# Row weights on ScalarE, and GpSimd's split of each expert's weights in pieces

## The chip, the core and the metric

The kernel runs on one core of one Trainium2 chip. The metric is the device time of one launch in microseconds (us). Three runs of the kernel before took 857.39, 860.36 and 863.71 us; their median is 860.36 us. The core has five engines that run their own instruction streams and meet through semaphores: TensorE (PE in the profile, its weight loads PEld), VectorE (DVE), ScalarE (ACT), GpSimd (POOL) and SyncE (SP), which here only issues transfers.

## The reference

Two blocks follow each other, each as `x = x + layernorm(block(layernorm(x)))`, on x of 2 x 2048 tokens by 256. The first is a gated linear attention with 16 heads. The second, around which the change is made, is a mixture of experts:

```
gate_out = x @ gate_w                       # 8 experts
top_v, top_i = top_k(gate_out, 2)           # each token goes to 2 of them
w = softmax over the two chosen, 0 elsewhere
def swiglu(x, w1, w2, w3):
    h = x @ w1
    return h * sigmoid(h) * (x @ w2) @ w3   # 256 -> 512 -> 256
out = sum over experts of swiglu(x, ew1[e], ew2[e], ew3[e]) * w[..., e]
out = out + swiglu(x, sw1, sw2, sw3)        # the shared expert
```

## The kernel before

**Two phases.** Phase A does the attention and the routing, and at its end each token's normalised row is scattered by GpSimd (L555) to a scratch in memory, sorted by expert. Phase B does the experts. It is a list of *units*: 5 shared units of 256 tokens, then 31 routed pairs (two tiles of 128 rows of one expert), 9 routed singles (one tile), and 11 more shared units. The table `tab`, written by VectorE (L1521 to L1523), tells each routed unit its expert and its first row. Experts come in rising order, about four pairs to each.

**Numbers in float16.** Each float32 matrix is kept as two float16 ones, a high and a low part, and each product is three matmuls. So each expert's weights are *split*: scaled into `wtmp_p` (L1695), copied to float16 (L1699), and the remainder computed (L1701). GpSimd does this for experts 1 to 8, 3072 columns per instruction. The scale comes from the largest weight of the expert: VectorE reduces each matrix (L1529, one per gap of its program), SyncE spreads the maxima over the partitions through memory, and VectorE's `scales` (L785 to L792) works out `w_scale`, for experts 2 and 3 in unit 2 and for 4 to 8 in unit 8.

**One unit.** TensorE turns the next unit's rows (L1269), computes the hidden layer in two halves (L1285, for a single L1305), then the output of the unit before (L1327). ScalarE takes the high part of the turned rows (`high_x`, L1386), applies SiLU (L1376), takes the high part of the gated product (`high_g`, L1369) and at the top of its next round moves output rows out of PSUM, each times its weight in `wrow` (`rows_out`, L1407). VectorE takes the low part of the rows (`low_x`, L1642), multiplies SiLU by the second product (`gated`, L1634) and takes the low part (`low_g`, L1625). The second matmul group of a half reuses the bank that `low_g` of two halves before has read.

**Row weights.** A scattered row carries its destination, the number of one of its two experts, a softmax value, and what to add to it where that number is this expert. ScalarE's `tags` (L1390, L1392) puts the destination and "number minus this expert" in `tag`. VectorE's `weights_of_rows` (L1574 to L1577) makes `wrow` of them in four small instructions, each behind the one before, right after `low_x` of the next unit.

**Queues.** SyncE loads the rows of a unit (L1206) once its expert is split and the row weights of the unit two before are written (`wrow_ready`). GpSimd scatters finished tiles back to memory (`scatter`, L1707 to L1716) in order; `ysh` has a ring of 28 tiles, so `rows_out` of tile j waits for the scatter of tile j - 28. GpSimd runs its program in written order: split 1, 2, 3, then 6 scatters after each of the splits 3 to 8, then the rest.

Of the kernel before, what the change touches and what calls it, by code (L numbers as in the profile page):

```python
# [5 lines left out]
ALU = mybir.AluOpType  # L6
# [11 lines left out]
def sandwich_kernel(nc, x, Wq, Wk, Wv, Wo, Wg, bg, gate_w, ew1, ew2, ew3, sw1, sw2, sw3, out):  # L18
    P = 128
# [19 lines left out]
    MW = KC * H  # L39
# [16 lines left out]
    with ctx:  # L56
# [167 lines left out]
        def settle(eng):  # L224


            eng.nop(nofuse=True)
# [828 lines left out]
        def sc(name, shape, dt=F32):  # L1056
            return phase_b.enter_context(nc.sbuf_tensor(name, shape, dt))
# [9 lines left out]
        second = sc("second", [P, 1])  # L1067
        chosen2 = sc("chosen2", [P, 2, 2])
        wrow = sc("wrow", [P, RT])
# [67 lines left out]
        def rows_upto(u):  # L1137

            return sum(t.tiles if t.routed else 1 for t in units[:u + 1])

        def halves_upto(u):
# [219 lines left out]
        def scalar_b(act):  # L1361
# [27 lines left out]
            def tags(t, e):  # L1389
# [3 lines left out]
                               bias=away9[:, e]).then_inc(T["tag_ready"], 1)  # L1393

            def rows_out(t, e):
                act.wait_ge(T["y_done"], t.u + 1)
# [37 lines left out]
            for u in range(ENDS):  # L1434
# [19 lines left out]
                if t is not None and t.halves == 2:  # L1454
                    high_g(t, 0)
                    silu(t, 1, e_of[u])
                    load_matrices()
                    high_g(t, 1)
            normalise_rows(C - 1)

        def vector_b(dve):
# [3 lines left out]
            def link(ins):  # L1465
                n[0] += 1
                ins.then_inc(T["late_chain"], 1)
                dve.wait_ge(T["late_chain"], n[0])
# [99 lines left out]

            def weights_of_rows(t, e):

                x = xt[t.q % 2]
                own, part, out = chosen2[:, 0, 0:t.tiles], chosen2[:, 1, 0:t.tiles], wrow[:, t.j:t.j + t.tiles]
                dve.wait_ge(T["tag_ready"], 2 * (t.q + 1))
                link(V.tensor_scalar(own, tag[:, t.j:t.j + t.tiles, 1], 0.0, None, ALU.is_equal))  # L1574
                link(V.tensor_tensor(part, own, x[:, 0:t.tiles, D + 3], ALU.mult))
                link(V.tensor_tensor(part, part, x[:, 0:t.tiles, D + 2], ALU.add))  # L1576
                V.tensor_scalar(out, part, w_scale[:, 2, e], None, ALU.mult).then_inc(T["wrow_ready"], 1)  # L1577

            def add_rows(c):
# [67 lines left out]
            for u in range(ENDS):  # L1647
# [4 lines left out]
                if prev is not None and prev.kind == "single":  # L1652
                    low_g(prev, 0)
                if following is not None and following.routed:
                    weights_of_rows(following, expert_of(dve, following))
                if waiting is not None:
# [30 lines left out]
        def pool_b(pool):  # L1687

            BETWEEN = 6

            def split(e):
                whole = W[:, e].rearrange("p m n -> p (m n)")
                if e > 1:
                    pool.wait_ge(experts_split, e - 1)
                pool.tensor_scalar(wtmp_p[:, :, :].rearrange("p m n -> p (m n)"), whole, w_scale[:, 1, e:e + 1], 1.0,  # L1695
                                   ALU.mult, ALU.mult).then_inc(T["pool_split"], 1)
                pool.wait_ge(T["pool_split"], 2 * e - 1)
                settle(pool)
                pool.tensor_copy(W16[:, e, :, 0, :], wtmp_p[:, :, :]).then_inc(T["pool_split"], 1)  # L1699
                pool.wait_ge(T["pool_split"], 2 * e)  # L1700
                pool.tensor_tensor(W16[:, e, :, 1, :], wtmp_p[:, :, :], W16[:, e, :, 0, :], ALU.subtract)\  # L1701
                    .then_inc(experts_split, 1)

            def scatter(j):
                need(pool, T["tag_ready"], 2 * (tile_unit[j].q + 1))
                need(pool, T["dest_ready"], j)
# [107 lines left out]
```

## Time and profile before

| | |
|---|---|
| three runs, median | 860.36 us |
| the profiled execution | 861.15 us |
| its span in the trace | 859.2 us |
| busy: PE, PEld | 740.7, 612.1 us |
| busy: DVE, ACT, POOL | 635.4, 415.6, 494.2 us |
| chain that ended last, by engine | PE 33%, DVE 18%, issue 5%, ACT 3%, POOL 1% |

Busy time of an engine is the time in which one of its compute instructions ran. PE is the busiest, but this is a mean over stages: phase B starts near 343 us, the routed units run from near 410 us to 752 us, and which engine sets the pace changes within them. The trace rows carry the start of an instruction, its duration, and in brackets how long its engine had been idle before and what ended the wait. The granted clock of PE is given as a share of full speed; where it is near 0.5 the clock was at 1.2 GHz, and at 1.00 it was at 2.4 GHz.

### The profile page before, as it was taken

The page shows a single profiled execution, that of the slowest core. Times are in us where ns is not written, and L with a number is a line of the kernel's source. Part 1 is how long each engine was busy: PE and PEld are TensorE (multiplying, and loading weights), DVE is VectorE, ACT ScalarE, POOL GpSimd, SP SyncE. Part 2 cuts the span into 40 slices and gives each one's busy share as a digit, 9 for nine tenths or more (in the row PEclk, how much of TensorE's full clock was granted, in tenths as well). Part 3 has the DMA queues.
Part 4 walks back from the last instruction along what each step waited for, and adds up shares of the span by engine and source line. Part 5 has one row for each costly group of instructions (what it writes and reads, how often), then busy time and mean ns, then how long its engine had stood idle before and what let it go on. Part 6 is the DMA issues. An engine that isn't in the chain of part 4 may idle for free.

```text
span 859.2 us, 25434 instructions
## 1 busy us (share of the span) xinstructions
PE 740.7 (86%) x8863; PEld 612.1 (71%) x8863; DVE 635.4 (74%) x1286; ACT 415.6 (48%) x840; POOL 494.2 (58%) x653
## 2 busy tenths in 40 slices
PE   5779989899899984867597889898999999999983
PEld 4557777787787763635486778787899985688873
DVE  4897989989998992778876766667555554547996
ACT  2645667566676542222234334433554444445553
POOL 4133335887778776689413877687534434325665
PEclk8999999999999996768799999999999999999998
DMA  7434333444453437662332111211212111217885
GB/s 245 99 80 104 102 101 82 151 120 114 137 158 108 130 109 249 208 178 74 92 106 78 51 45 57 76 45 50 76 57 76 57 51 59 79 48 219 196 169 102
DMA packets 57480, 93.24 MB, mean 109 GB/s; under 512 B 7216, under 2 KB 35760, under 8 KB 57360
## 3 DMA queue, kind: packets, MB, share of 16 engines
q1 hardware_dynamic: 40512, 60.66, 24.8%
q0 software_dynamic: 10672, 22.57, 9.7%
q10 hardware_dynamic: 6176, 8.40, 3.6%
q8 instruction: 77, 1.26, 0.6%
q14 instruction: 43, 0.35, 0.1%
HBM read 59.60 MB, written 32.01 MB: 107 GB/s over the span
## 4 chain that ended last, share of the span: by engine, by line
PE 33%; DVE 18%; issue 5%; ACT 3%; POOL 1%; DVEq 1%; DMA 1%; ACTq 0%; POOLq 0%
PE bank L1285 19%; PE bank L1327 10%; DVE chosen L1576 4%; DVE wpart L1529 2%; PE bank L1305 2%; DVE bank L1634 2%; ACT gh L1369 2%; DVE gl L1625 1%; DVE wtmp_p L1588 1%; DVE chosen L1574 1%; PE bank L1269 1%; DVEq L1168 1%; DVE wmax L786 1%; DVE stc L1601 1%; ACT xh L1386 1%
## 5 line engine op out<-in xcount | busy, mean ns | idle before, releaser
L1285 PE MATMUL bank<-xh,W 128*128 128x256 f16 x1504 | 271.9, 282 | 47.9 <-DVE gl L1625 41.0
L1285 PE MATMUL bank<-xl,W 128*128 128x256 f16 x752 | 211.8, 282 | 1.5 <-issue 1.5
L1285 PEld LDWEIGHTS bank<-xh,W 128*128 (+1 forms) x1504 | 151.7, 101 | 76.1 <-issue 41.5
L1716 POOL DMA_INDIRECT yt_scratch<-ysh,dest x71 | 76.4, 1076 | 161.8 <-ACT ysh L1407 124.6
L1369 ACT ACTIVATE gh<-bank 128x512 f16<-128x512 f32 x103 | 61.3, 595 | 223.0 <-DVE bank L1634 214.5
L1327 PE MATMUL bank<-W,gh 128*128 (+1 forms) x824 | 141.3, 276 | 3.0 <-DVE gl L1625 1.9
L1625 DVE TENSOR_TENSOR gl<-bank,gh 128x512 f16<-128x512 f32 x103 | 71.0, 689 | 66.9 <-ACT gh L1369 66.3
L1327 PE MATMUL bank<-W,gl 128*128 (+1 forms) x412 | 113.8, 276 | 0.3 <-issue 0.3
L555 POOL DMA_INDIRECT xs_scratch<-xn_all,posi x64 | 88.5, 1382 | 27.5 <-issue 13.9
L1634 DVE SCALAR_TENSOR_TENSOR bank<-sl,w_scale,bank 128x512 f32<-128x512 f32 x94 | 70.8, 753 | 35.5 <-PE bank L1285 19.5
L607 PE MATMUL bank<-xnT,wT 128*128 128x256 f32 x384 | 94.2, 397 | 2.3 <-ACT xnT L369 2.3
L1327 PEld LDWEIGHTS bank<-W,gh 128*128 128x128 f16 x824 | 81.4, 99 | 16.3 <-issue 2.9
L607 PEld LDWEIGHTS bank<-xnT,wT 128*128 128x128 f32 x384 | 72.5, 195 | 18.9 <-issue 5.8
L1285 PEld LDWEIGHTS bank<-xl,W 128*128 (+1 forms) x752 | 75.9, 101 | 12.2 <-issue 1.9
L1376 ACT ACTIVATE sl<-bank,w_scale 128x512 f32<-128x512 f32 x103 | 70.6, 685 | 19.0 <-PE bank L1285 11.8
L850 DVE TENSOR_TENSOR_SCAN W<-W,diag 128x1024 f32<-128x1024 f32 x32 | 72.1, 2281 | 10.2 <-DMA W<-gate_scratch 9.9
L1642 DVE TENSOR_TENSOR xl<-bank,xh 128x512 f16<-128x512 f32 (+1 forms) x40 | 25.2, 631 | 37.5 <-ACT xh L1386 35.7
L711 PE MATMUL bank<-W 64*32 64x64 f32 x2048 | 35.3, 224 | 16.0 <-DVE W L870 9.1
L1701 POOL TENSOR_TENSOR W<-wtmp_p,W 128x3072 f16<-128x3072 f32 x8 | 48.4, 6048 | 0.7
L1327 PEld LDWEIGHTS bank<-W,gl 128*128 128x128 f16 x412 | 40.8, 99 | 6.4 <-issue 1.3
L420 ACT ACTIVATE W<-qT,qmask 128x512 f32<-128x512 f32 x64 | 42.4, 711 | 5.5 <-DVE qT L904 5.5
L1407 ACT ACTIVATE ysh<-bank,wrow 128x256 f32<-128x256 f32 x71 | 30.2, 471 | 30.4 <-PE bank L1327 27.1
(205 smaller groups left out, 1412.6 us busy)
## 6 DMA issues: line engine op xcount, KB each, us to landing
W<-gate_scratch SPq DMA_DIRECT2D x64, 256.0 KB
ysh<-yt_scratch SPq DMA_DIRECT2D x16, 512.0 KB, 4.6
xt<-xs_scratch SPq DMA_DIRECT2D x31, 260.0 KB
W<-in_L_ffn_ew_dram ACTq DMA_DIRECT2D x15, 512.0 KB, 3.7
W<-in_L_ffn_ew_dram SPq DMA_DIRECT2D x9, 512.0 KB, 8.3
x_in<-in_L_attn_x_dram SPq DMA_DIRECT2D x16, 256.0 KB, 3.6
out_dram<-x SPq DMA_DIRECT2D x16, 256.0 KB
xT_scratch<-xn2T SPq DMA_DIRECT2D x16, 256.0 KB
```

What stands on the lines that cost most here:

```text
L420: act.activation(free3(qx[s % 2][:, c]), free3(qT[s % 2][:, :, :, :]), ACT.Copy, scale=qmask[:, c:c + 1]).then_inc(S["qx_ready"], 1)
L555: pool.indirect_dma_start(xs_d[:, :], bass.IndirectOffsetOnAxis(ap=posi[:, s, b * TOPK + k:b * TOPK + k + 1], axis=0), xn2[s % XB][:, b, : ...
L607: last = mm(dst[:, g * B * P:(g + 1) * B * P], wT[:, n, k, g * P:(g + 1) * P], xnT[s % 2][:, k, :], start=(k == 0), stop=(k == KC - 1))
L850: V.tensor_tensor_scan(dec[:, w, :], gbc[s % 2][:, w, :], free2(diag[:, :, :]), 0.0, ALU.mult, ALU.add).then_inc(S["decay_ready"], 1)
L1285: last = mm(dst[n % 2][:, i * R:(i + 1) * R], W16[:, e, m, s, at:at + P], a[:, k, :], start=(k == 0 and s == 0 and a is x_h), stop=(k == K ...
L1327: last = mm(pYB[t.u % 2][:, r * D:(r + 1) * D], g[:, i, r, :], W16[:, e, 2, s, c * D:(c + 1) * D], start=(c == 0 and r == 0 and a is gh an ...
L1369: act.activation(gh[t.u % 2][h][:, :], (pH1 if t.kind == "single" else pH2)[n % 2][:, :], ACT.Copy)\
L1376: act.activation(sl[n % 2][:, :], pH1[n % 2][:, :], ACT.Silu, scale=w_scale[:, 0, e])\
L1625: V.tensor_tensor(gl[t.u % 2][h][:, :], (pH1 if t.kind == "single" else pH2)[n % 2][:, :], gh[t.u % 2][h][:, :], ALU.subtract).then_inc(T[ ...
L1634: V.scalar_tensor_tensor((gg if t.kind == "single" else pH2)[n % 2][:, :], sl[n % 2][:, :], w_scale[:, 1, e], pH2[n % 2][:, :], ALU.mult, ...
L1701: pool.tensor_tensor(W16[:, e, :, 1, :], wtmp_p[:, :, :], W16[:, e, :, 0, :], ALU.subtract)\
L1716: pool.indirect_dma_start(yt_d[:, :], bass.IndirectOffsetOnAxis(ap=dest[:, j:j + 1], axis=0), ysh[:, ETILES + j % RING, :], None).then_inc ...
```

## The change

`weights_of_rows` goes from VectorE to ScalarE, as five or four small ACTIVATE instructions: |number - e|, then max(0, 1 - that), which is 1 where the number is this expert and 0 else, then one multiply-add for each tile, then the product with the expert's scale. They stand at the end of ScalarE's round, behind the last `high_g`. The counts on `tag_ready` are adapted (`tags_upto`). GpSimd's split is cut: three scalings and three casts of 1024 columns, six subtractions of 512. `BETWEEN` goes from 6 to 2.

```
+            def weights_of_rows(t, e):
+
+                x, done = xt[t.q % 2], tags_upto(t.q - 1)
+                far, own, part = chosen2[:, 0, 0:t.tiles], chosen2[:, 1, 0:t.tiles], chosen2[:, 2, 0:t.tiles]
+                act.wait_ge(T["tag_ready"], done + 2)
+                need(act, T["wrow_ready"], t.q)
+                act.activation(far, tag[:, t.j:t.j + t.tiles, 1], ACT.Abs).then_inc(T["tag_ready"], 1)
+                act.wait_ge(T["tag_ready"], done + 3)
+                act.activation(own, far, ACT.Relu, scale=-1.0, bias=1.0).then_inc(T["tag_ready"], 1)
+                act.wait_ge(T["tag_ready"], done + 4)
+                for r in range(t.tiles):
+                    act.activation(part[:, r:r + 1], x[:, r, D + 3:D + 4], ACT.Identity, scale=own[:, r:r + 1],
+                                   bias=x[:, r, D + 2:D + 3]).then_inc(T["tag_ready"], 1)
+                act.wait_ge(T["tag_ready"], tags_upto(t.q))
+                act.activation(wrow[:, t.j:t.j + t.tiles], part, ACT.Copy, scale=w_scale[:, 2, e])\
+                   .then_inc(T["wrow_ready"], 1)
...
                     high_g(t, 1)
+                if following is not None and following.routed:
+                    weights_of_rows(following, e_of[u + 1])
...
-            def weights_of_rows(t, e):
-
-                x = xt[t.q % 2]
-                own, part, out = chosen2[:, 0, 0:t.tiles], chosen2[:, 1, 0:t.tiles], wrow[:, t.j:t.j + t.tiles]
-                dve.wait_ge(T["tag_ready"], 2 * (t.q + 1))
-                link(V.tensor_scalar(own, tag[:, t.j:t.j + t.tiles, 1], 0.0, None, ALU.is_equal))
-                link(V.tensor_tensor(part, own, x[:, 0:t.tiles, D + 3], ALU.mult))
-                link(V.tensor_tensor(part, part, x[:, 0:t.tiles, D + 2], ALU.add))
-                V.tensor_scalar(out, part, w_scale[:, 2, e], None, ALU.mult).then_inc(T["wrow_ready"], 1)
...
-            BETWEEN = 6
+            BETWEEN = 2
...
-                pool.tensor_scalar(wtmp_p[:, :, :].rearrange("p m n -> p (m n)"), whole, w_scale[:, 1, e:e + 1], 1.0,
-                                   ALU.mult, ALU.mult).then_inc(T["pool_split"], 1)
...
-                pool.tensor_copy(W16[:, e, :, 0, :], wtmp_p[:, :, :]).then_inc(T["pool_split"], 1)
...
-                pool.tensor_tensor(W16[:, e, :, 1, :], wtmp_p[:, :, :], W16[:, e, :, 0, :], ALU.subtract)\
-                    .then_inc(experts_split, 1)
+                for m in range(3):
+                    pool.tensor_scalar(wtmp_p[:, m, :], W[:, e, m], w_scale[:, 1, e:e + 1], 1.0,
+                                       ALU.mult, ALU.mult).then_inc(T["pool_split"], 1)
+                for m in range(3):
+                    pool.wait_ge(T["pool_split"], done + 3 + m)
+                    settle(pool)
+                    pool.tensor_copy(W16[:, e, m, 0, :], wtmp_p[:, m, :]).then_inc(T["pool_split"], 1)
+                for m in range(3):
+                    pool.wait_ge(T["pool_split"], done + 4 + m)
+                    for k in range(2):
...
+                        pool.tensor_tensor(W16[:, e, m, 1, half], wtmp_p[:, m, half], W16[:, e, m, 0, half],
+                                           ALU.subtract).then_inc(experts_split if last else T["pool_split"], 1)
```

On ScalarE, the round of an early pair, from `high_g` of its second half to `high_x` of the unit after the next; before:

```order
L1369 ACTIVATE gh_1<-bank 128x512
L1407 ACTIVATE ysh<-bank,wrow 128x256 x2
L1168 TENSOR_LOAD tab
L1168 ISA x2
L1386 ACTIVATE xh<-bank 128x512
```

and with the change:

```order
L1373 ACTIVATE gh_1<-bank 128x512
L1405 ACTIVATE chosen<-tag 128x2
L1407 ACTIVATE chosen<-chosen 128x2
L1410 ACTIVATE chosen<-xt,chosen 128x1 x2
L1413 ISA
L1413 ACTIVATE wrow<-chosen,w_scale 128x2
L1428 ACTIVATE ysh<-bank,wrow 128x256 x2
L1172 TENSOR_LOAD tab
L1172 ISA x2
L1390 ACTIVATE xh<-bank 128x512
```

The weights' instructions now stand between `high_g` and the moving out of rows, ahead of `high_x`. On GpSimd, from the split of expert 3 to that of expert 4, with the change:

```order
L1707 TENSOR_SCALAR wtmp_p<-W,w_scale 128x1024 x3
L1712 CAST W<-wtmp_p 128x1024 x3
L1720 TENSOR_TENSOR W<-wtmp_p,W 128x512 x6
L1726 TENSOR_SCALAR second<-tag 128x1
L1729 TENSOR_SCALAR dest<-tag,spare,second 128x1
L1735 DMA yt_scratch<-ysh,dest 9216x256
L1726 TENSOR_SCALAR second<-tag 128x1
L1729 TENSOR_SCALAR dest<-tag,spare,second 128x1
L1735 DMA yt_scratch<-ysh,dest 9216x256
```

Before, a split was three instructions of 3072 columns, and six scatters stood where two stand now.

## Rows read from the trace of the kernel before

**Rows 1.** Windows: busy us (and count) per engine, PE clock, DMA share, GB/s.
```profile
380.00:420.00 40.00, 25.67 (x184) 19.57 (x182) 34.85 (x30) 7.35 (x14) 36.44 (x12) 0.80 0.26 74
464.00:610.00 146.00, 131.25 (x1136) 114.67 (x1137) 99.84 (x138) 60.70 (x140) 108.98 (x105) 0.95 0.19 56
610.00:700.00 90.00, 90.00 (x826) 81.12 (x825) 47.17 (x99) 43.60 (x97) 37.74 (x66) 1.00 0.21 64
```
**Rows 2.** Timeline, split of expert 4: start us, us, engine, line, operation.
```profile
470.85 2.83 POOL L1695 TENSOR_SCALAR wtmp_p<-W,w_scale 128x3072 f32<-128x3072 f32 x1
...
476.65 6.01 POOL L1701 TENSOR_TENSOR W<-wtmp_p,W 128x3072 f16<-128x3072 f32 x1
476.82 5.86 DVE L1576 TENSOR_TENSOR chosen<-chosen,xt 128x2 f32<-128x2 f32 x1
...
485.94 0.39 PE L1285 MATMUL bank<-xh,W 128*128 128x256 f16 x1 [3.06 <-DVE gl L1625]
```
**Rows 3.** Timeline, split of expert 2: a DVE instruction with a PSUM operand beside it.
```profile
399.58 6.34 POOL L1701 TENSOR_TENSOR W<-wtmp_p,W 128x3072 f16<-128x3072 f32 x1
...
401.20 0.75 DVE L1634 SCALAR_TENSOR_TENSOR bank<-sl,w_scale,bank 128x512 f32<-128x512 f32 x1
```
**Rows 4.** Timeline, DVE and PE during the splits of experts 1 and 2.
```profile
381.68 2.05 DVE L1521 TENSOR_SCALAR tab<-tb 1x64 int32<-1x64 f32 x1
...
387.03 5.67 DVE L786 TENSOR_SCALAR wmax<-wmax 128x2 f32<-128x2 f32 x1
...
393.61 0.76 DVE L1634 SCALAR_TENSOR_TENSOR bank<-sl,w_scale,bank 128x512 f32<-128x512 f32 x1
...
395.78 0.39 PE L1285 MATMUL bank<-xh,W 128*128 128x256 f16 x1 [5.80 <-DVE gl L1625]
...
396.88 3.16 DVE L1642 TENSOR_TENSOR xl<-xsT,xh 128x512 f16<-128x512 f32 x1
```
**Rows 5.** Timeline, DVE and PE during the split of expert 3.
```profile
409.28 0.69 DVE L1642 TENSOR_TENSOR xl<-bank,xh 128x512 f16<-128x512 f32 x1 [1.58 <-issue]
...
418.11 1.21 DVE L1529 TENSOR_REDUCE wpart<-W 128x1 f32<-128x1024 f32 x1
...
421.61 0.39 PE L1285 MATMUL bank<-xh,W 128*128 128x256 f16 x1 [8.68 <-DVE gl L1625]
```
**Rows 6.** Timeline, DVE's `gated` of the first halves between two splits.
```profile
519.55 0.76 DVE L1634 SCALAR_TENSOR_TENSOR bank<-sl,w_scale,bank 128x512 f32<-128x512 f32 x1 [0.62 <-PE bank L1285]
...
526.43 0.76 DVE L1634 SCALAR_TENSOR_TENSOR bank<-sl,w_scale,bank 128x512 f32<-128x512 f32 x1 [0.62 <-issue]
```
**Rows 7.** ACT: two dependent instructions (timeline); small and two-operand ones (ns min/median/max).
```profile
156.14 0.59 ACT L387 ACTIVATE rneg<-bank 128x512 f32<-128x512 f32 x1
156.76 0.63 ACT L390 ACTIVATE ef<-rneg 128x512 f32<-128x512 f32 x1
...
L1392 ACT ACTIVATE tag<-xt,away x40: 282/302/314, 409.2 to 742.7; 128x2 f32<-128x2 f32 x31, 128x1 f32<-128x1 f32 x9
...
L1417 ACT ACTIVATE lnc<-wtmp_p,shiftc,rsc x22: 584/587/603, 786.3 to 854.3; 128x256 f32<-128x256 f32 x22
```
**Rows 8.** Timeline, an early pair: ACT's `high_x`, DVE's `low_x`, next reduction.
```profile
434.63 0.60 ACT L1386 ACTIVATE xh<-bank 128x512 f16<-128x512 f32 x1
...
436.04 0.69 DVE L1642 TENSOR_TENSOR xl<-bank,xh 128x512 f16<-128x512 f32 x1
...
437.81 1.22 DVE L1529 TENSOR_REDUCE wpart<-W 128x1 f32<-128x1024 f32 x1 [0.16 <-issue]
```
**Rows 9.** POOL: a subtraction-like instruction of 512 columns (ns); two scatters in a row.
```profile
L574 POOL TENSOR_TENSOR x<-ln_o,x_in x16: 1259/1328/1548, 56.5 to 333.4; 128x512 f32<-128x512 f32 x16
...
643.73 1.07 POOL L1716 DMA_INDIRECT yt_scratch<-ysh,dest  x1 [2.77 <-ACT ysh L1407]
...
646.39 1.06 POOL L1716 DMA_INDIRECT yt_scratch<-ysh,dest  x1 [0.79 <-POOL dest L1710]
```
**Rows 10.** Waits of PE in the singles, 708 to 752 us: us, times, longest.
```profile
PE bank L1313 <- DVE gg L1634: 0.9, 2, 0.6
```

More of the change, by code:

```diff
@@ L1067, in sandwich_kernel @@
         second = sc("second", [P, 1])
-        chosen2 = sc("chosen2", [P, 2, 2])
+        chosen2 = sc("chosen2", [P, 3, 2])
         wrow = sc("wrow", [P, RT])
@@ L1139, in rows_upto, with tags_upto @@
             return sum(t.tiles if t.routed else 1 for t in units[:u + 1])
+        def tags_upto(q):
+            return sum(4 + t.tiles for t in routed[:q + 1])
         def halves_upto(u):
@@ L1653, in vector_b @@
                     low_g(prev, 0)
-                if following is not None and following.routed:
-                    weights_of_rows(following, expert_of(dve, following))
                 if waiting is not None:
@@ L1687, in pool_b @@
         def pool_b(pool):
-            BETWEEN = 6
+            BETWEEN = 2
             def split(e):
-                whole = W[:, e].rearrange("p m n -> p (m n)")
+                done = 11 * (e - 1)
                 if e > 1:
                     pool.wait_ge(experts_split, e - 1)
-                pool.tensor_scalar(wtmp_p[:, :, :].rearrange("p m n -> p (m n)"), whole, w_scale[:, 1, e:e + 1], 1.0,
-                                   ALU.mult, ALU.mult).then_inc(T["pool_split"], 1)
-                pool.wait_ge(T["pool_split"], 2 * e - 1)
-                settle(pool)
-                pool.tensor_copy(W16[:, e, :, 0, :], wtmp_p[:, :, :]).then_inc(T["pool_split"], 1)
-                pool.wait_ge(T["pool_split"], 2 * e)
-                pool.tensor_tensor(W16[:, e, :, 1, :], wtmp_p[:, :, :], W16[:, e, :, 0, :], ALU.subtract)\
-                    .then_inc(experts_split, 1)
+                for m in range(3):
[8 more added lines that the diff above has]
+                    for k in range(2):
+                        half = slice(k * MW // 2, (k + 1) * MW // 2)
+                        last = m == 2 and k == 1
+                        if last:
+                            pool.wait_ge(T["pool_split"], done + 11)
+                        pool.tensor_tensor(W16[:, e, m, 1, half], wtmp_p[:, m, half], W16[:, e, m, 0, half],
+                                           ALU.subtract).then_inc(experts_split if last else T["pool_split"], 1)
             def scatter(j):
-                need(pool, T["tag_ready"], 2 * (tile_unit[j].q + 1))
+                need(pool, T["tag_ready"], tags_upto(tile_unit[j].q - 1) + 2)
                 need(pool, T["dest_ready"], j)
```

## The prediction

> **What bounds the kernel now.** I read the windows first. From 610 to 700 us TensorE is busy for 90.00 of 90 us at full clock and executes 826 matmuls, 0.109 us each; a pair unit has 76 (48 of the hidden layer, 24 of the output, 4 to turn rows), so it takes 8.28 us and TensorE sets the pace [rows 1]. From 464 to 610 us the same kind of unit runs, but 1136 matmuls took 146 us. At 0.109 they need 123.8. 22.2 us are lost there, as idle time and as the low clock behind it (granted 0.95 in the mean). From 380 to 420 us TensorE is busy for only 25.7 of 40 us, and VectorE for 34.9.
>
> Then the timeline, at one loss. GpSimd begins the split of expert 4 at 470.85; its subtraction runs from 476.65 to 482.66. VectorE's third weights instruction, on 128x2 numbers, starts at 476.82 and takes 5.86 us: it ends when the subtraction does [rows 2]. TensorE then waits 3.06 us for `low_g`, queued behind it on VectorE. So a tiny instruction stops VectorE for as long as a GpSimd instruction lasts. It does not happen to every VectorE instruction: beside the subtraction of expert 2, `gated`, with an operand in PSUM, took its 0.75 us [rows 3]. Those stopped have their operands in SBUF alone: L1576, L1521, L786, and `low_x` of a shared unit, 3.16 us [rows 2, 4]. `low_x` of a routed unit reads PSUM and took 0.69 [rows 5].
>
> The Trainium skill ("SBUF — State Buffer", section "SBUF: two separate sides") says that VectorE and GpSimd share a pair of ports as an exclusive lock, held for a whole instruction, and that VectorE wants it with two SBUF inputs or in a two-port mode. By that rule, the trace agrees: 5.86 us against 0.75 us.
>
> **The change, part by part.** All savings are counted against the profiled execution, 861.15 us, which is 0.8 us above the median of the runs.
>
> *Splits of experts 4 to 8 (464 to 610 us).* In the pairs VectorE's only SBUF-alone work is the row weights (the scales of 4 to 8 are done before split 4). They leave, so nothing on VectorE can be stopped, whatever GpSimd does. Of the 22.2 us, part lies ahead of 470.85, where the window opens on the low clock after a wait for the maxima of these experts; that wait stays. I give it half of an average stall, 2.2 us. **Saved: 20.0 us** (17 if the waits leave small ones behind, 21 if not).
>
> *Split of expert 3.* `low_x` ends at 409.97; the next reduction, with the weights between them, starts at 418.11 [rows 5]. Without them it starts at once, 8.1 us earlier. TensorE waited 8.68 us for this chain, so it all counts. **Saved: 8.1 us.**
>
> *Splits of experts 1 and 2.* From 381.68 to `gated` at 393.61 VectorE executes nine SBUF-alone instructions (table and scales) in 11.9 us, two of which lasted 2.05 and 5.67 us, and TensorE waits 5.80 us for what follows [rows 4]. These stay; GpSimd's instructions beside them get shorter. A piece of 512 columns costs 1.33 us [rows 9] against 6.01 for 3072 [rows 2], so 1.83 ns a column and 0.39 us fixed. A third of the scaling is 2.83/3 plus at most 0.26, near 1.15 us. A split becomes 12 pieces in about 15 us instead of 11.8. If VectorE gets one instruction in at each end of a piece, the nine end near 391.9: 1.7 us saved. Bounds: all of TensorE's wait, 5.8, if two go through at an end; and a loss of 3.2 (the longer split) if the ports do not change hands between pieces. I take 1.7, from the pieces' own durations. `low_x` at 396.88 is held for at most 1.33 instead of 2.47 us, but TensorE had little idle time there: 0.5 (0 to 1). **Saved: 2.2 us.** Expert 1's rows are loaded some 3 us later (the split ends at 396 instead of 393); their `low_x` starts only at 409.28 [rows 5], which hides it.
>
> *Weights on ScalarE.* A ScalarE instruction that waits for the one before starts 0.03 us after its end (156.14 + 0.59, then 156.76) [rows 7]. A small one with one pointer takes 0.30. One of 256 columns with two pointers takes 0.587; at (0.63 - 0.30)/510 = 0.65 ns a column, some 0.42 of that is fixed. So: 0.25 for the first, which has no pointer, 0.30 for the second, 0.42 and 0.30 for the two multiply-adds, whose ends overlap, 0.30 for the last, and three waits of 0.03: W = 1.65 us. Ends: 1.3 (all overlapped) and 3.9 (each self-wait as on GpSimd, 0.79 [rows 9], instead of 0.03).
>
> Behind it on ScalarE stand `rows_out`, `high_x` and SiLU of the next unit. Where TensorE sets the pace, the round has room: between two splits, catching up, VectorE's `gated` came every 6.88 us [rows 6]. VectorE gives back about 1.0 (low_x's end at 436.73 to the reduction at 437.81 [rows 8], register load included), ScalarE adds 1.65: 7.5 us, under 8.28. Cost: nothing, until W = 2.4.
>
> In the first four pairs (about 420 to 460 us) VectorE sets the pace, with three reductions in each unit. There `high_x` ends at 435.23 and `low_x` starts at 436.04, so 0.81 us of slack [rows 8]; with 1.65 more on ScalarE it starts 0.84 late, and VectorE gains 1.08 behind it. The 0.2 us are within what I can resolve: **0**, ends +3 and -4.
>
> The skill speaks against this part ("ScalarE: Activation LUTs", section "Rules for kernel authors"): additions, products and relu belong on VectorE. By that rule the weights would stay, and with them the stops of up to 5.86 us each; no run here shows both engines doing them.
>
> *Singles.* TensorE waits 0.9 us for `gated`, queued behind the weights on VectorE [rows 10]. That goes; ScalarE does them while it waits for the output. **Saved: 0.9 us.**
>
> *Fewer scatters between splits.* From split 4 to 8: five splits of 15 us and ten scatters of 2.66 us [rows 9] are about 100 us, in which 24 tiles come and 10 go. The backlog of some 16 to 18 tiles is under the ring's 28, and 2.66 against 4.14 us a tile clears it before the singles end. Splits finish earlier than before, and units wait for none. Cost and gain: nothing. Cover: the 10 free tiles.
>
> **Sum.** 20.0 + 8.1 + 2.2 + 0.9 = 31.2 us. 861.15 - 31.2 = 830.0; less the 0.8 us, **829 us** as a median. Behind the singles nothing changes; it only starts earlier.
>
> **Rivals.**
> *The ports stay with GpSimd from piece to piece* (18%). Then the table and the scales are held for the whole, longer split: 829 + 1.7 + 3.2 = 834 us. For: scalings follow each other with no wait. Against: L1521 ended near 383.7 and L786 began at 387.03, so VectorE did get instructions in while one split ran [rows 4]. The page on SBUF leaves it open (whoever starts first).
> *The early part gains all it can* (10%): 829 - 4.1 = 825 us.
> *ScalarE's round becomes a mild bound* (8%), W = 2.8: 8.68 a unit, 0.4 x 27 pairs, and 1.15 x 4 in the first pairs: 844 us. For: five instructions, one behind the other, 40 times. Against: the 0.03.
> *ScalarE's chain sets the pace outright, and the kernel is slower* (3%). Place: between `high_g` and `rows_out`. W = 3.9 gives 6.88 - 1.0 + 3.9 = 9.8 a pair, 1.5 x 27 + 2.3 x 4 = 50 us: 879 us. It decides from W = 3.3, where all is lost; slower by 1% from 3.6. Against it: the same 0.03.
> *The ring fills* (2%): only if a split took over 24 us, as 12 pieces each with a long wait would; `rows_out` then waits, about 839 us.
> *It does not do what it says* (4%): the stops move to another VectorE instruction, such as `low_x`, and the time stays near 857. Against: rows 3 and 5.
> My forecast has 55%.
>
> **Range and chances.** 821 to 840 us reaches from the second rival's mirror, 825, less the upper ends of the terms, to the first, 834, plus their lower ends; it leaves out the mild and the outright bound on ScalarE and the failure. A change under 1%, 8.6 us, cannot be told from none. Faster by over 1%: 55 + 18 + 10 + 8 + 2 = 93%; within it 4%; slower 3%.
>
> **What would show it.** PE clock 1.00 and PE busy throughout from about 455 to 690 us, with no wait for `low_g` over 0.5 us; no VectorE instruction over 1.4 us beside a split; `gated` every 8.28 us; ScalarE's five instructions within 1.3 to 2.0 us; GpSimd's split near 15 us and its scatters without idle time until near 680 us. The prediction is wrong if ScalarE's weights take over 2.4 us, or if VectorE's scales last over 10 us.

## The result, and the profile after

Four runs of the changed kernel on one chip took 820.49, 822.92, 833.32 and 818.72 us (median 821.7), four of the kernel before 853.3 to 863.71 (median 858.88). The ratio of the times is 0.956 (95% interval 0.948 to 0.964). Ratios and their intervals leave out runs over 1.5% slower than the fastest of their kernel, such as that of 833.32; the medians keep them. The forecast was 829, range 821 to 840. In this comparison the two medians lie 37.2 us apart, 6 more than the 31.2 that I had worked out. The two later comparisons gave 29.9 and 27.7 us. Over all its 14 runs, in three comparisons, the median of the changed kernel is 825.6 us; over the 36 runs of the kernel before, in five, it is 856.6, and the difference is 31.0.

The profiled execution took 820.49 us, span 818.6. The same windows as in [rows 1], shifted with the work (us, then busy time and count of PE, PEld, DVE, ACT, POOL, PE clock, DMA share, GB/s):

```profile
380.00:420.00 40.00, 35.94 (x297) 29.53 (x297) 30.30 (x35) 15.95 (x38) 38.30 (x35) 0.94 0.38 120
455.00:600.00 145.00, 145.00 (x1330) 130.75 (x1329) 62.91 (x88) 91.72 (x246) 111.20 (x151) 1.00 0.22 65
600.00:690.00 90.00, 89.68 (x766) 75.54 (x765) 37.23 (x55) 57.80 (x164) 48.05 (x86) 1.00 0.23 71
```

From 455 to 600 us TensorE is busy for 145.00 of 145 us at clock 1.00, 0.109 us a matmul. GpSimd's splits of experts 4 to 8 end at 531.6 us, and beside them TensorE now keeps the pace that it had before only from 610 us on. Its waits from 455 to 700 us (us in total, times, longest) are one:

```profile
PE bank L1309 <- DVE gl L1638: 0.3, 1, 0.3
```

The split of expert 4 on GpSimd, which answers to [rows 2]:

```profile
442.50 3.30 POOL L1707 TENSOR_SCALAR wtmp_p<-W,w_scale 128x1024 f32<-128x1024 f32 x3 [10.71 <-DVE w_scale L792]
445.93 3.37 POOL L1712 CAST W<-wtmp_p 128x1024 f16<-128x1024 f32 x3
449.27 6.85 POOL L1720 TENSOR_TENSOR W<-wtmp_p,W 128x512 f16<-128x512 f32 x6
```

Twelve pieces, 13.6 us (I had said about 15; before it was 11.8). It also begins earlier in the program than before, since two scatters stand ahead of it and not six. VectorE at the table and the scales, and the answer to [rows 4]:

```profile
377.27 0.17 DVE L1544 TENSOR_SCALAR tab<-tb 1x64 int32<-1x64 f32 x1
...
378.30 3.46 DVE L786 TENSOR_SCALAR wmax<-wmax 128x2 f32<-128x2 f32 x1
...
382.00 0.94 DVE L789 TENSOR_SCALAR w_scale<-wmax 128x2 f32<-128x2 f32 x1
...
383.17 0.92 DVE L791 TENSOR_TENSOR w_scale<-w_scale 128x2 f32<-128x2 f32 x1
...
384.21 0.76 DVE L1647 SCALAR_TENSOR_TENSOR bank<-sl,w_scale,bank 128x512 f32<-128x512 f32 x1
...
387.48 1.68 DVE L1655 TENSOR_TENSOR xl<-xsT,xh 128x512 f16<-128x512 f32 x1
```

L786 was held for 3.46 us, over all three scalings (378.43 to 381.73); L789 and L791 by one cast each. So one of my signs failed: I had said that no VectorE instruction would last over 1.4 us beside a split. The nine instructions took 6.9 us instead of 11.9, and `low_x` 1.68 instead of 3.16. ScalarE's weights of a pair:

```profile
404.82 0.20 ACT L1405 ACTIVATE chosen<-tag 128x2 f32<-128x2 f32 x1
405.04 0.20 ACT L1407 ACTIVATE chosen<-chosen 128x2 f32<-128x2 f32 x1
405.28 0.66 ACT L1410 ACTIVATE chosen<-xt,chosen 128x1 f32<-128x1 f32 x2
406.09 0.30 ACT L1413 ACTIVATE wrow<-chosen,w_scale 128x2 f32<-128x2 f32 x1
406.29 0.67 ACT L1431 ACTIVATE ysh<-bank,w_scale 128x512 f32<-128x512 f32 x1
```

From the first to the next instruction W = 1.47 us (forecast 1.65). The scatters, as in [rows 9]: GpSimd issues one every 2.63 us and waits for ScalarE by more than 0.8 us again only from about 645 us on (I had said near 680):

```profile
639.64 1.07 POOL L1735 DMA_INDIRECT yt_scratch<-ysh,dest  x1 [0.79 <-POOL dest L1729]
...
642.27 1.06 POOL L1735 DMA_INDIRECT yt_scratch<-ysh,dest  x1 [0.79 <-POOL dest L1729]
...
646.32 1.07 POOL L1735 DMA_INDIRECT yt_scratch<-ysh,dest  x1 [2.21 <-ACT ysh L1428]
```

**Where the time went, by stage.** I cut each trace at events that every kernel has on VectorE: the first instruction of the table; the second `gated` of unit 2 and the first of unit 3 (shared units); `low_x` of the first routed pair; the reduction after it; the first `gated` three pairs later; that of the first single; that of the first late shared unit; the end. Each column is the difference of two start times, in us. The forecast's terms A, B and E are, in its order, the splits of experts 1 and 2, of 3, and of 4 to 8.

```
               table  to    to    low_x  reduc- gated  gated   gated  to     table
               begins gated gated pair   tion   pairs  single  late   end    to end
               at     ---- term A ----   B             E       singles
before         381.7  11.93  7.59  8.08  8.83   44.08  249.44  44.83  102.74  477.5
  again (e4)   376.8   5.38 10.56  8.08  8.17   44.40  249.10  44.82  102.62  473.1
  again (e12)  380.7  13.09  7.59  8.09  8.83   44.70  248.21  44.83  102.68  478.0
  again (e16)  388.4   5.39 10.57  8.58  7.67   44.50  248.78  44.82  102.75  473.1
changed        377.3   6.94  6.12  8.08  0.61   44.03  229.15  43.45  102.95  441.3
  again (e9)   382.4   5.85  5.12 10.46  0.61   44.07  229.16  43.45  102.73  441.5
  again (e14)  386.2   5.83  5.12 10.45  0.61   43.87  229.23  43.45  102.73  441.3
```

Between the two first profiles lie 40.6 us of span: 36.2 from the table on, 4.4 ahead of it, where nothing was changed. Over four executions of the kernel before and three of the changed one the part from the table on is 475.4 us (473.1 to 478.0) against 441.4 (441.3 to 441.5): **from the table on, the change is worth 34 us**. The table itself begins at 381.9 us in the mean of the four and at 382.0 in that of the three.

### The profile page after: what moved, and what is told of

Its sections match the earlier page's. It is cut to its first block, busy times and chain, and to the rows that moved or that the text cites. A ratio compares the mean times of both kernels' runs of the same rounds, so it can differ in the third digit from the quotient of the medians.

```text
span 818.6 us, 25472 instructions
## 1 busy us (share of the span) xinstructions
PE 722.8 (88%) x8863; PEld 603.3 (74%) x8863; DVE 561.9 (69%) x1126; ACT 461.8 (56%) x1031; POOL 505.0 (62%) x725
## 4 chain that ended last, share of the span: by engine, by line
PE 39%; DVE 11%; issue 5%; ACT 2%; POOL 1%; DMA 1%; DVEq 0%; ACTq 0%; POOLq 0%
PE bank L1289 22%; PE bank L1331 12%; PE bank L1309 3%; DVE wpart L1552 2%; PE bank L1273 2%; DVE bank L1647 2%; DVE wtmp_p L1601 1%; DVE gl L1638 1%; ACT gh L1373 1%; DVE stc L1614 1%; DMA spread_b<-largest_scratch 1%; DVE shiftc L1631 0%; DVE wmax L786 0%; DVE xl L1655 0%; PE bank L1317 0%
## 5 line engine op out<-in xcount | busy, mean ns | idle before, releaser
L1289 PE MATMUL bank<-xh,W 128*128 128x256 f16 x1504 | 263.7, 277 | 20.1 <-DVE gl L1638 13.2
L1289 PE MATMUL bank<-xl,W 128*128 128x256 f16 x752 | 208.1, 277 | 1.7 <-issue 1.7
L1289 PEld LDWEIGHTS bank<-xh,W 128*128 (+1 forms) x1504 | 149.2, 99 | 46.4 <-issue 20.0
L1331 PE MATMUL bank<-W,gh 128*128 (+1 forms) x824 | 138.4, 273 | 3.1 <-DVE gl L1638 1.9
L1720 POOL TENSOR_TENSOR W<-wtmp_p,W 128x512 f16<-128x512 f32 x48 | 54.6, 1166 | 0.6
L711 PEld LDWEIGHTS bank<-W 64*32 64x32 f32 x2048 | 28.7, 106 | 24.1 <-issue 11.8
```

The lines of the kernel that those rows point to most:

```text
L711: last = mm(pY[u][r * 32:(r + 1) * 32, col:col + TS], vpu[s % 2][own, u, b, g * GH + 2 * r + even, lo:lo + 2 * DH], probs[own, b, w, c, g, ...
L1289: last = mm(dst[n % 2][:, i * R:(i + 1) * R], W16[:, e, m, s, at:at + P], a[:, k, :], start=(k == 0 and s == 0 and a is x_h), stop=(k == K ...
L1331: last = mm(pYB[t.u % 2][:, r * D:(r + 1) * D], g[:, i, r, :], W16[:, e, 2, s, c * D:(c + 1) * D], start=(c == 0 and r == 0 and a is gh an ...
L1720: pool.tensor_tensor(W16[:, e, m, 1, half], wtmp_p[:, m, half], W16[:, e, m, 0, half], ALU.subtract).then_inc(experts_split if last else T ...
```

## The experiments

**e1 and e2: either half alone.** e1 moves the weights to ScalarE and leaves the split whole; e2 cuts the split and leaves the weights on VectorE. Both keep `BETWEEN` at 6.

```
 e1:  weights_of_rows on ScalarE, as in the change
      pool.tensor_scalar / tensor_copy / tensor_tensor   3072 columns each, as before
 e2:  weights_of_rows on VectorE, as before
+     for m in range(3): ... 1024 columns / 1024 / 2 x 512, as in the change
```

> The row weights on ScalarE, GpSimd's split whole as before, six scatters between splits. Theory A (the move of the weights alone removes the stops of VectorE in the pairs): the pairs from 464 us on lose nothing, the split of expert 3 neither; the splits of experts 1 and 2 stop VectorE as before. Saved 20 + 8 + 1.5 = about 29 us against before, ratio 0.963 to 0.970. Theory B (the pieces carry a good part of it in the pairs as well): under 20 us saved, and TensorE still waits for low_g beside the splits of experts 4 to 8.

> The split in pieces, the weights still on VectorE, six scatters. Theory A with ports that change hands at each end of a piece: of the weights' three SBUF-alone instructions beside a split each is held for at most one piece (1.1 to 1.2 us), a stop of some 3.5 us in place of 7.5, so about 10 to 15 us saved in all, ratio 0.982 to 0.989. If the ports do not change hands between pieces that follow without a wait: each stop stays near 7 us, and nothing is saved or up to 5 us lost, ratio 0.995 to 1.006.

e1 took 826.75 us (813.35 to 831.11), e2 831.54 (824.83 to 839.45; ratio to before 0.978, 0.970 to 0.986), the kernel before 855.59 beside them. From the table to the end e1 has 446.9 us, 28.6 less than the kernel before, as expected (about 29). e2 has 450.3, 25.2 less, where I had expected 10 to 15. The stages (columns of the table above) tell more:

```
e1             376.2  13.39  7.60  8.08  0.61   43.61  227.56  43.45  102.56
e2             372.8   9.02  5.11  9.17  4.42   47.13  227.93  44.94  102.54
```

In the pairs beside the later splits *each half alone* brings all of the 20 us (E: 227.6 and 227.9); the two do not add up. TensorE's window from 460 to 600 us, e1 first, then e2, is full in both:

```profile
460.00:600.00 140.00, 140.00 (x1284) 126.25 (x1283) 61.43 (x86) 89.66 (x245) 109.84 (x108) 1.00 0.22 63
```
```profile
460.00:600.00 140.00, 140.00 (x1285) 126.19 (x1283) 89.26 (x154) 67.09 (x154) 110.51 (x144) 1.00 0.20 61
```

The forecast credited E to the weights' move, and that is enough; that stops cut to about 1 us vanish in the slack of a round as well, it did not see. Term A comes from the pieces alone: e1 keeps 29.1 us there, e2 has 23.3. With the split whole, VectorE in e1 stands where it stood before:

```profile
376.24 3.52 DVE L1544 TENSOR_SCALAR tab<-tb 1x64 int32<-1x64 f32 x1
...
380.04 2.65 DVE L1546 SCALAR_TENSOR_TENSOR tab<-tb 1x64 int32<-1x64 f32 x1
...
383.05 5.66 DVE L786 TENSOR_SCALAR wmax<-wmax 128x2 f32<-128x2 f32 x1
```

and B needs the weights gone to be whole: e2 keeps 4.42 of the 8.83 us. In the early pairs e2 is 2.7 us worse than the mean of the kernel before (47.1 against 44.4); why was not followed up.

**e3: the order of the scatters.**

```
-            BETWEEN = 2
+            BETWEEN = 6
```

> The changed kernel with six scatters between splits, as before. Theory A: the order of scatters is worth nothing (both orders keep GpSimd ahead of what waits for it): the time of the changed kernel within 0.4%, ratio to before 0.951 to 0.962. Rival C (experts split earlier save something of their own, since units waited for them): slower than the changed kernel by 4 us or more.

816.7 us (814.51 to 830.5; ratio 0.955, 0.948 to 0.963), from the table to the end 440.2 us (changed: 441.3). No difference, as forecast: the third part of the change is worth nothing by itself.

**e4, e12, e16: the kernel before, again.** No edit.

> The kernel before, once more with a profile. The start of VectorE's L1521 lay at 381.68 us in the trace of before and its counterpart at 377.27 us in that of the changed kernel, in code that the change does not touch. If that is the spread of single executions, this run has it anywhere between 376 and 384 us, and the stop from there to gated at 393.61 (11.9 us) changes by some us with how VectorE and GpSimd happen to stand to each other. If it is the changed kernel's own, it lies within 0.5 us of 381.7.

> The kernel before once more, one look. Theory: from the first table instruction to low_x of the last leading shared unit 24 to 28 us (27.6 and 24.0 so far), because which of VectorE's small instructions meets which of GpSimd's long ones changes from run to run; the table starts later where the granted clock from 340 to 375 us is lower. Rival (the stage is 27.6 and the 24.0 was the exception): 27 to 28 us again. Span 845 to 860 us.

> The kernel before, a fourth profile. Theory: from the table to low_x of the last leading shared unit 24 to 29 us, never under 23; from the table to the end 473 to 478.5 us, so 32 to 37 us more than the changed kernel, with 35 in the mean; the table starts where the granted clock from 340 to 375 us puts it. Rival (the start of the table and not that stage makes the difference): under 472 us from the table to the end.

851.77, 860.57 and 863.57 us. Their rows stand in the table. Term A's stage takes two shapes. In the first profile and e12 the scales ran beside the subtraction (L786 5.67 us, L791 5.83). In e4 and e16 they got by with one stop, and `low_x` of the shared unit met the subtraction instead. e4:

```profile
378.62 3.41 DVE L791 TENSOR_TENSOR w_scale<-w_scale 128x2 f32<-128x2 f32 x1
...
385.42 6.13 DVE L1642 TENSOR_TENSOR xl<-xsT,xh 128x512 f16<-128x512 f32 x1
```

Over the four the stage is 26.2 us (24.0 to 28.8), over the three of the changed kernel 21.3 (21.1 to 21.4). e12's 28.8 lies a little over the 24 to 28 expected. A is worth 4.9 us, and what one pair of profiles shows depends on where the executions fell (6.5 in the first). Part of this stage is the clock that follows a wait. In e9 TensorE waited 3.42 us, and then, busy for 6.00 of 6 us, executed 33 matmuls at a granted clock of 0.55; seven us later it executed 58 at 1.00:

```profile
391.00:397.00 6.00, 6.00 (x33) 4.31 (x32) 5.23 (x7) 1.53 (x3) 6.00 (x6) 0.55 0.49 138
398.00:404.00 6.00, 6.00 (x58) 5.41 (x56) 1.94 (x3) 1.47 (x6) 5.57 (x6) 1.00 0.36 89
```

In the first profile of the changed kernel the clock was back at 1.00 from 385.3 us on. This fits the third column, which has 8.08 us there and 10.46 and 10.45 in e9 and e14.

**e5 and e10: a gap between the pieces.** Each piece of a split waits for the one before, which is to leave the ports free for a moment; e5 with the weights on VectorE (e2's kernel), e10 in the changed kernel.

```
+                    if m:
+                        pool.wait_ge(T["pool_split"], done + m)
+                        settle(pool)
...
+                        pool.wait_ge(T["pool_split"], done + 6 + 2 * m + k)
+                        settle(pool)
```

> The weights on VectorE, pieces as in e2_pieces, but now each scaling and each subtraction of a split also waits for the one before it. In e2_pieces VectorE got in at the end of every cast and every subtraction, but instructions that met the three scalings lasted until the third ended (4.06, 1.60, 2.08 us). Theory H (the ports change hands where GpSimd waits between two instructions): no SBUF-alone VectorE instruction lasts over 1.4 us beside a split, those beside scalings among them. Rival (scalings keep the ports for another reason): some still last over 1.6 us beside scalings. The pairs cost 228 us from gated of unit 8 to the first single, as in e2_pieces, since 1.1 us stops are absorbed.

> The changed kernel, but each of GpSimd's pieces waits for the one before, so that the ports are free for a moment between any two. Theory (a VectorE instruction is held over several scalings only because they follow each other without a gap): no SBUF-alone instruction of VectorE beside a split lasts over 1.5 us (3.46 us in the changed kernel); the stage from the table to low_x of the last leading shared unit takes 19.5 to 21 us; a split is 1 to 2 us longer, which nothing waits for; time within 2 us of the changed kernel. Rival (the longer split holds up the first units): the stage takes over 21.5 us and the kernel is 2 to 4 us slower.

e5 took 829.45 us (826.92, 831.98; ratio 0.964, 0.956 to 0.972), e10 818.16 (815.03 to 821.26). In e2, without gaps, VectorE's third table instruction was held to the end of the third scaling:

```profile
373.29 4.06 DVE L1523 SCALAR_TENSOR_TENSOR tab<-tb 1x64 int32<-1x64 f32 x1
```
```profile
373.97 3.30 POOL L1696 TENSOR_SCALAR wtmp_p<-W,w_scale 128x1024 f32<-128x1024 f32 x3
377.42 3.38 POOL L1701 CAST W<-wtmp_p 128x1024 f16<-128x1024 f32 x3
```

It had started 0.68 us before the first scaling, while GpSimd issued a scatter; what held it until then is not shown. In e10 no stop lasts over 1.03 us, and the table and the scales take 5.56 us (6.94, 5.85 and 5.83 in the changed kernel's three profiles):

```profile
375.39 1.12 POOL L1710 TENSOR_SCALAR wtmp_p<-W,w_scale 128x1024 f32<-128x1024 f32 x1
376.69 1.11 POOL L1710 TENSOR_SCALAR wtmp_p<-W,w_scale 128x1024 f32<-128x1024 f32 x1 [0.18 <-POOL wtmp_p L1710]
377.97 1.12 POOL L1710 TENSOR_SCALAR wtmp_p<-W,w_scale 128x1024 f32<-128x1024 f32 x1 [0.17 <-POOL wtmp_p L1710]
```
```profile
376.84 1.03 DVE L1546 SCALAR_TENSOR_TENSOR tab<-tb 1x64 int32<-1x64 f32 x1
...
378.23 0.88 DVE L786 TENSOR_SCALAR wmax<-wmax 128x2 f32<-128x2 f32 x1
```

A gap of 0.17 us lets VectorE in; none between scalings does not. In e5 two stops last longer than the 1.4 us that I had allowed (1.48 and 1.73 us). Each is over at the end of one scaling, but had begun 0.31 and 0.57 us before it, again while GpSimd issued a scatter.

Subtractions need no gap. In e2 they follow each other without one, and VectorE gets one instruction in at the end of each:

```profile
408.74 5.60 POOL L1709 TENSOR_TENSOR W<-wtmp_p,W 128x512 f16<-128x512 f32 x5
```
```profile
409.95 1.07 DVE L1575 TENSOR_TENSOR chosen<-chosen,xt 128x2 f32<-128x2 f32 x1
411.06 1.07 DVE L1576 TENSOR_TENSOR chosen<-chosen,xt 128x2 f32<-128x2 f32 x1
```

The whole of term A's stage in e10 is 20.8 us, 0.5 less than in the changed kernel, and from the table to the end 440.7 against 441.4. The mechanism is there, and is worth next to nothing. E in e5 is 227.9 us, as in e2.

**e6 and e7: more work in ScalarE's weights,** 3 and 8 further dependent copies. e7:

```
-            return sum(4 + t.tiles for t in routed[:q + 1])
+            return sum(4 + 8 + t.tiles for t in routed[:q + 1])
...
+                for k in range(8):
+                    act.wait_ge(T["tag_ready"], done + 4 + t.tiles + k)
+                    act.activation(part, part, ACT.Copy).then_inc(T["tag_ready"], 1)
```

> The changed kernel with three more small dependent copies in ScalarE's weights of each routed unit; their result is the same. Each costs 0.23 us (0.20 and 0.03 from its end to the next start), so 0.69 a unit. The catching-up round was 7.07 us in the changed kernel (gated at 450.11 and 457.18), so 1.21 us are free below 8.28. Expected: pairs unchanged at 228 to 230 us from gated of unit 8 to the first single; the stage before it, from the reduction to gated of unit 8, 44.0 us now, 1 to 3 us longer, since there each us on ScalarE delays low_x. If ScalarE's chain is already on the path in the pairs, they take 27 x 0.69 = 19 us more.

> Eight more such copies: 1.84 us a unit, a round of 7.07 + 1.84 = 8.9 us against TensorE's 8.28. Expected: the pairs take about 0.63 x 27 = 17 us more (245 us in place of 229), the stage before up to 7 us more. If the threshold that I forecast (ScalarE's weights at 2.4 us in all) does not exist, the pairs stay at 229 us.

e6: 820.56 us; e7: 865.44. In e6 W was 2.17 us (560.24 to 562.41), and the first halves' `gated` came every 8.30 us as before: nothing lost in the later pairs. The early pairs took 45.97 us, 2.0 more than the changed kernel's mean, within the 1 to 3 expected. In e7:

```profile
562.77 0.20 ACT L1405 ACTIVATE chosen<-tag 128x2 f32<-128x2 f32 x1
...
563.92 1.85 ACT L1414 ACTIVATE chosen<-chosen 128x2 f32<-128x2 f32 x8
...
566.12 0.82 ACT L1431 ACTIVATE ysh<-bank,wrow 128x256 f32<-128x256 f32 x2
```

W = 3.35, and a pair took 8.95 us. TensorE's waits from 460 to 700 us now name the rows' transfer, which SyncE issues once the weights are written:

```profile
PE bank L1273 <- DMA xt<-xs_scratch: 12.8, 21, 1.4
PE bank L1289 <- DVE gl L1641: 2.7, 2, 2.1
```

The runs put the bound between W = 2.17, where nothing is lost, and 3.35. A pair's 8.95 us is 0.65 over 8.30, which gives 3.35 - 0.65 = 2.7 us; E's stage, 28 pairs, lost 22.5 us, 0.80 a pair, which gives 2.55. So my estimate is 2.5 to 2.7 us (forecast 2.4), about 1 us above the change's own W. Of the 45 us lost, 10.5 lie ahead of the table; 22.5 fall in E's stage (17 expected), 6.5 in the early pairs (up to 7 expected), 5.0 in the singles, which I had not expected. From the table to the end e7 takes 475.9 us against 475.4 in the kernel before: at W = 3.35 all is lost, as forecast for 3.3.

**e8: the weights earlier in ScalarE's round,** behind the SiLU of the first half, where ScalarE waits anyway.

```
+                early = t is not None and t.halves == 2
+                if early and following is not None and following.routed:
+                    weights_of_rows(following, e_of[u + 1])
...
-                if following is not None and following.routed:
+                if following is not None and following.routed and not early:
```

> The changed kernel with ScalarE's weights moved in its round: behind the SiLU of the first half, where it idles for VectorE (2.7 to 3 us in the early pairs), in place of behind the last high_g; singles as they are. high_x is no longer behind the weights, so low_x of the early pairs starts 0.8 to 0.9 us earlier: 3 us less from the reduction to gated of unit 8 (41 in place of 44 us), the pairs unchanged at 229 us. If ScalarE's high_g is delayed by them instead (weights 1.47 us against an idle time of under 1 us while catching up), the pairs stay the same too, since the round still has room. Against the changed kernel 2 to 3.5 us, 0.3%, under what times can tell; the stage in the trace tells.

820.42 us (815.76 to 828.8; ratio 0.951, 0.943 to 0.958). The early pairs' stage fell from 44.0 to 41.6 us (41 expected), and the whole from the table on from 441.4 to 438.2. There the weights at the end of the round do cost what VectorE gets back: the forecast's 0 was a balance, not an absence. One wait is left, in the fourth pair:

```profile
440.60 1.31 DVE L785 TENSOR_REDUCE wmax<-spread_b 128x5 f32<-128x640 f32 x1 [2.57 <-DMA spread_b<-largest_scratch]
```

**e11, e13, e15: without that wait.** The scales of experts 4 to 8 two gaps later on VectorE; e11 and its repetition e13 with e8's edit, e15 alone. e9 and e14 are the changed kernel on the same chips.

```
-                elif turn == SCALES2:
+                elif turn == SCALES2 + 2:
```

> The changed kernel itself, again, as the yardstick for the next two on the same chip. Theory (term A was too small, and the rest of the miss is where an execution stands when the table is written): from the first table instruction to low_x of the last leading shared unit 20.0 to 21.5 us (21.1 in the changed kernel's first profile, 27.6 in that of the kernel before); the table starts anywhere from 373 to 388 us, later where the granted clock from 340 to 375 us is lower (so far 0.74 gave 387.8 and 0.89 gave 372.8), and median 817 to 823 us. Rival (the scales' stage itself scatters as widely): that stage lands above 23 us here.

> The version with ScalarE's weights behind the SiLU of the first half, and the scales of experts 4 to 8 two gaps later on VectorE. Theory (in the fourth early pair VectorE waits 2.57 us for the spread maxima, and TensorE 2.8 us behind it): that wait goes, the stage from the last reduction of the early pairs to the first half of unit 8 takes 39 instead of 41.6 us, TensorE's wait for low_g from 435 to 470 us falls from 3.3 to under 1 us, and the kernel gains 2 to 3 us, 816 to 819 us. Rival (the later start of the split of expert 4, by about 5 to 8 us, makes its rows late or puts the splits beside slower work): TensorE waits for the rows of expert 4 or the gain is given back, 819 to 823 us.

> The version with the weights behind the SiLU of the first half and the scales of experts 4 to 8 two gaps later, again, beside the changed kernel. Theory: from the first table instruction to the end 434 us (433.9 in its first profile, 441.3 and 441.5 in the changed kernel), so 7 us under the changed kernel in the median of the same chip, 812 to 818 us. Rival (the first profile was a lucky one): 438 us or more, and no difference that the timed runs show.

> The changed kernel once more. Theory: from the table to the end 441 to 442 us, from the table to low_x of the last leading shared unit 20.5 to 21.5 us; the start of the table lies where the granted clock from 340 to 375 us puts it: near 377 us at 0.85, near 381 us at 0.80. Rival (the start scatters for another reason): a start off that line by over 4 us. Median 818 to 824 us.

> The changed kernel with nothing but the scales of experts 4 to 8 two gaps later. Theory (VectorE's wait for the spread maxima, 2.57 us, and TensorE's 2.8 us behind it go, whatever the place of the weights): from the table to the end 437 us, 4 us less than the changed kernel; the weights' earlier place gives the other 3 us. Rival (both edits are needed together): 440 us or more.

In e11 the reduction starts at once, and TensorE's wait for `low_g` from 430 to 700 us is down to 1.0 us:

```profile
449.11 1.31 DVE L785 TENSOR_REDUCE wmax<-spread_b 128x5 f32<-128x640 f32 x1
```

From the table to the end: 433.9 us in e11, 433.8 in e13, 437.2 in e15, against 441.4. So 4.2 us are the later scales', 3.3 the earlier weights'. The gain lies in the stage that I had named, and is larger there: the early pairs take 36.1 us in e11 (41.6 in e8, 39 expected) and 40.0 in e15 (44.0 in the changed kernel). E's stage is 230.0 and 229.3. Of the 5.5 us between e8 and e11, 1.1 go again in E's stage. Timed, e15's one run took 818.33 us. e11 took 817.79 us (812.7 to 824.08) beside 825.05 (811.63 to 825.64) for the changed kernel (e9), and e13 817.65 (806.62 to 821.98; ratio to before 0.961, 0.955 to 0.967) beside 827.73 (823.94 to 829.38; 0.971, 0.966 to 0.977) in e14. The medians of e9 and e14 lie over what I had expected of the changed kernel (817 to 823 and 818 to 824). The version of e11 and e13 beats both kernels: from the table on by 7.5 us the changed one, and the timed runs of e13 and e14 do not overlap.

e14 also shows how far executions lie apart before the change is reached. Windows of e13 and then e14:

```profile
300.00:340.00 40.00, 20.59 (x387) 16.85 (x388) 23.76 (x74) 14.83 (x30) 26.25 (x45) 0.78 0.64 209
340.00:375.00 35.00, 28.11 (x212) 21.84 (x213) 28.84 (x56) 8.29 (x14) 26.50 (x32) 0.89 0.67 205
```
```profile
300.00:340.00 40.00, 30.62 (x594) 23.95 (x593) 27.10 (x74) 14.18 (x30) 27.08 (x41) 0.90 0.43 131
340.00:375.00 35.00, 20.50 (x151) 16.79 (x152) 20.61 (x57) 10.23 (x19) 22.02 (x33) 0.73 0.66 223
```

The table begins at 370.8 us in e13 and at 386.2 in e14. I had expected it to follow the clock of the second window, and over 18 traces it does (correlation -0.94). But the first window of e14 has the higher clock and the more matmuls: the whole end of phase A is shifted, and the fixed window catches another part of it. The last pair of scans of the attention starts at 303.2 us in e13 and at 313.6 in e14, so 10.4 of the 15.4 us were there by then. That reading of mine is not shown; the spread arises within phase A, and why is open.

## Why the prediction was off, step by step

- **Term A failed** (splits of experts 1 and 2): 2.2 us forecast, 6.5 between the first two profiles, 4.9 over seven. I gave VectorE one instruction at each end of a piece and let the nine end 1.7 us earlier, and took 0.5 for `low_x`. The nine end 5.0 us earlier in the first profiles and 2.7 over all. Two things were wrong. Where scalings follow each other without a gap VectorE gets none in (3.46 us), yet each cast and each subtraction lets it in after about 0.9 to 1.1 us. And the split before is a matter of meeting: part of what the scales escape, `low_x` gets (6.13 us in e4). I had priced one meeting from one execution. The bounds, -3.2 and +5.8 with up to 1 for `low_x`, held.
- **The first comparison's miss, added up.** The spans of the first two profiles differ by 40.6 us, 9.4 more than 31.2: 4.4 lie ahead of the table, where nothing was changed, 4.3 in A, 0.5 in the singles, 0.4 in B and E, and the other stages take 0.2 back. So about half of it was the chance of these two executions.
- **The sum's base.** The 31.2 us were taken off one execution of the kernel before, and its medians were 858.9, 855.6, 860.5, 855.0 and 855.4 us in the five comparisons, its single runs 842.7 to 869.6. The table's start alone scatters over 17.6 us (370.8 to 388.4, 18 traces). The low end of 821 had no room for this. It did not even hold the terms' own ends: 825 less 1 (E), 0.5 (`low_x`) and 4 (early pairs) is 819.5.
- **E** (20.0): 20.3 in the first profiles, 19.7 over all. Right in size; the reason was half of it, since e2 gets it with the weights still on VectorE.
- **B** (8.1): 8.2, and 7.8 over all. TensorE's wait was VectorE's chain, as read.
- **Early pairs** (0): 0.05 between the first profiles, 0.4 over all. It was a balance, as written: e8 takes ScalarE's side of it away and gains 2.4. **Singles** (0.9): 1.4. **Fewer scatters** (0): nothing (e3).
- **W** (1.65 us): 1.47 us. The bound, put at 2.4, is 2.5 to 2.7 by estimate, and between 2.17 and 3.35 by e6 and e7.
- **Rivals.** The ports stay with GpSimd from piece to piece: true among the three scalings, false for the rest. ScalarE as a bound: not at W = 1.5 to 2.2. The ring did not fill: ScalarE waited for no scatter from 380 to 740 us. The second rival, the early part gains all it can (825 us), came nearest: it puts A at 6.3 us, and A was 6.5 between the first profiles, 4.9 over all.

With A at 4.9 and the other terms as measured the sum is 34 us; off the kernel before's own 856.6 that is 822.6, between the changed kernel's median in the first comparison (821.7) and over all (825.6). That the medians over all differ by 31.0 us, almost the 31.2 forecast, is luck: the trace has 34 from the table on, and the 3 us between the two are within the spread ahead of the table.

## What to carry to other kernels

When a small VectorE instruction with its operands in SBUF lasts as long as a GpSimd instruction beside it, shorten the GpSimd instruction or move the small one. Where TensorE sets the pace, one of the two suffices once the stop fits into the round's slack (E, in e1 and e2); where VectorE sets it, each stop that is left counts (B, in e2). Price a stop that depends on a meeting over several executions, not one, and look at what runs next to the long instruction when the first victim has gone. Compare two profiles from a mark just ahead of the change, not from their start: here that took the spread of the changed kernel's three profiles from 8.9 us (818.6 to 827.5) down to 0.2. Check that the mark is the same event in every version: in e11 the first `gated` behind the scales, at 452.43 us, is two `gated` later than before, and taken as the mark it would have put the gain into E's stage (222.3 us instead of 230.0).

## What the runs showed of the hardware

- Three GpSimd scalings of 1024 columns, issued without a wait between them, kept a waiting VectorE instruction out until the last had ended (3.46 us here, 4.06 in e2, 3.89 in e9). Subtractions of 512 columns (1.15 us), back to back too, let it in at the end of each (1.07 to 1.09 us in e2). Casts of 1024 columns did as well (0.92 to 0.94 us), but here each cast waits for the one before (0.13 us from the end of one to the start of the next in the changed kernel), so they do not test the case without a gap. With a gap of 0.17 us scalings let it in too. What tells scalings from subtractions is open.
- The Trainium skill ("SBUF — State Buffer", section "SBUF: two separate sides") has the lock held for a whole instruction. The casts and subtractions agree (0.92 to 1.09 us, one of them each); beside scalings without a gap VectorE was held over three (3.46 us).
- Dependent ACTIVATEs on 128x2 take 0.22 to 0.24 us from start to start, wait included (404.82, 405.04, 405.28); eight in a row 1.85 us in e7.
